# Attention and mixture of experts: second norm moved to DVE, pairs routed an iteration earlier, shared down products at the end on the output's PSUM banks

## The reference, cut to what matters

```python
x = x + attention(layernorm(x), ctx)              # 16 heads of 16, causal
h = layernorm(x)                                  # the second norm
scores = sigmoid(h @ gate_w.T)                    # 32 experts in 8 groups
# best 4 groups, best 8 experts of them; weights normalised, times 2.5
routed = sum_e weight_e * (silu(h @ w_gate_e) * (h @ w_up_e)) @ w_down_e
shared = (silu(h @ sh_gate.T) * (h @ sh_up.T)) @ sh_down.T     # two experts for all
out = x + routed + shared
```

## Time and profile before

| | |
|---|---|
| median of 3 runs | 600.98 us (599.45 to 603.95) |
| the profiled execution | 597.24 us, span 595.4 us |
| busy: PE, DVE, ACT, POOL | 455.0, 335.6, 208.9, 387.5 us |
| granted TensorE clock, mean | 0.858 |
| DMA | 85.08 MB, mean 143 GB/s |

### The profile page before, as it was taken

One profiled execution on the slowest core, in us unless ns is written; L12 is line 12 of the kernel. 1 busy time (PEld: TensorE's weight loads), 2 busy tenths in 40 slices (PEclk: granted clock), 3 DMA queues, 4 the chain that ended last, 5 costly groups with the idle time before them and its releaser, 6 DMA issues.

```text
span 595.4 us, 11968 instructions
## 1 busy us (share of the span) xinstructions
PE 455.0 (76%) x3114; PEld 344.2 (58%) x3114; DVE 335.6 (56%) x977; ACT 208.9 (35%) x595; POOL 387.5 (65%) x321
## 2 busy tenths in 40 slices
PE   2987996897585745971819998999989999998513
PEld 2985674665454523541507777777668867776302
DVE  5984999888867724531204555555546555555324
ACT  3452563343332300100004444444435544444201
POOL 7560122478877787757724888888868888888800
PEclk9998998866876756885858999999989999999955
DMA  6377600122222269389535888889888989888686
GB/s 206 94 286 224 224 4 2 30 80 79 68 79 80 78 197 395 93 231 252 159 97 96 146 144 139 143 141 145 140 132 142 146 138 151 144 141 138 82 243 210
DMA packets 88352, 85.08 MB, mean 143 GB/s; under 512 B 29164, under 2 KB 78956, under 8 KB 88288
## 3 DMA queue, kind: packets, MB, share of 16 engines
q0 software_dynamic: 27056, 32.01, 31.9%
q1 hardware_dynamic: 58928, 49.92, 30.2%
q10 hardware_dynamic: 2304, 2.37, 1.5%
HBM read 40.44 MB, written 43.80 MB: 141 GB/s over the span
## 4 chain that ended last, share of the span: by engine, by line
POOL 30%; issue 23%; PE 18%; DVE 11%; DMA 9%; SPq 8%; ACT 1%; POOLq 0%
POOL chosen_rows L365 21%; PE ps L971 7%; POOL sum L382 5%; DMA sum<-out_rows,rows 4%; DMA weight<-chosen_rows 3%; PE ps L987 3%; SPq L219 3%; POOL rec L356 2%; PE ps L749 2%; PE ps L963 2%; DVE prob L568 2%; SPq L299 2%; SPq L300 2%; DVE xn L514 1%; SPq L308 1%
## 5 line engine op out<-in xcount | busy, mean ns | idle before, releaser
L382 POOL DMA_INDIRECT sum<-out_rows,rows x131 | 202.1, 1542 | 61.0 <-issue 32.8
L365 POOL DMA_INDIRECT chosen_rows<-rec,dest x128 | 127.9, 999 | 43.0 <-issue 40.8
L971 PE MATMUL ps<-w_all,hx 128*128 x524 | 138.6, 388 | 0.0
L704 DVE SCALAR_TENSOR_TENSOR opened_t<-th,ps 128x128 f32<-128x128 f32 x131 | 37.7, 287 | 128.1 <-ACT th L475 127.2
L971 PEld LDWEIGHTS ps<-w_all,hx 128*128 128x128 f32 x524 | 91.2, 194 | 7.5
L987 PE MATMUL ps<-w_all,ax 128*128 x262 | 84.5, 404 | 1.6 <-ACT ax L481 0.9
L963 PE MATMUL ps<-cst,rows 128*128 128x128 f32 x262 | 53.1, 285 | 24.9 <-DMA weight<-chosen_rows 23.7
L471 ACT ACTIVATE hx<-ps 128x256 f32<-128x256 f32 x131 | 50.2, 383 | 35.5 <-PE ps L963 34.6
L475 ACT ACTIVATE th<-ps 128x128 f32<-128x128 f32 x131 | 36.3, 277 | 66.9 <-PE ps L971 66.4
L987 PEld LDWEIGHTS ps<-w_all,ax 128*128 128x128 f32 x262 | 43.8, 190 | 25.1 <-issue 21.0
L963 PEld LDWEIGHTS ps<-cst,rows 128*128 128x128 f32 x262 | 31.9, 144 | 43.3 <-DMA weight<-chosen_rows 35.5
(11 more groups left out here) (148 smaller groups left out, 670.1 us busy)
## 6 DMA issues: line engine op xcount, KB each, us to landing
rows<-chosen_rows SPq DMA_DIRECT2D x131, 128.5 KB
w_all<-w_exp SPq DMA_DIRECT2D x6, 1536.0 KB, 12.4
w_all<-sum SPq DMA_DIRECT2D x12, 384.0 KB, 7.1
sum<-pad_rec SPq DMA_DIRECT2D x2, 1600.0 KB
chosen_rows<-pad_rec SPq DMA_DIRECT2D x17, 144.5 KB, 6.2
chosen_rows<-pad_rec ACTq DMA_DIRECT2D x16, 144.5 KB, 5.3
w_all<-w_exp SPq DMA_DIRECT2D x1, 2304.0 KB, 12.7
weight<-chosen_rows SPq DMA_DIRECT2D x131, 0.5 KB
```

Source lines behind the costliest of these rows:

```text
L365: pool.indirect_dma_start(out=recs, out_offset=bass.IndirectOffsetOnAxis(ap=dest[:, B, r:r + 1], axis=0), in_=rec[:, B, :], in_offset=None ...
L382: pool.indirect_dma_start(out=sums[n], out_offset=bass.IndirectOffsetOnAxis(ap=rows[:, i % NROW, TOKEN:TOKEN + 1].bitcast(U32), axis=0), i ...
L704: v.scalar_tensor_tensor(opened_t[:, n, :], th[:, n, :], 1.0, ps[:, 2 + n, 0:FI], ALU.add, ALU.mult).then_inc(t_open, 1)
L971: last = t.matmul(ps[:, 2 + i % 2, 0:D].rearrange("p (a n) -> p a n", n=P), hx[:, i % 3, k * P:(k + 1) * P], weights(i)[:, k:2 * KC:2, :], ...
```

## The change

1. The second norm's subtraction and product go from POOL to DVE, behind `outputs_scaled` of the same step. POOL keeps the power. `send(B)` now follows the power of batch B+4. The token numbers in `rec` are written once ahead of the loop.
2. `route` runs at even steps from 4 on, `places` at even steps from 6 on, and PE's `count` at odd steps. The loop is one step shorter.
3. PE's transposes of `rec` go into the turning of batch B+3's probabilities, onto the free ends of banks 4 and 5; ACT copies them out between two probability copies. The residual waits no longer for the copy of the batch ahead.
4. The shared experts' down products and their additions on DVE go away from the middle. `sh_act` keeps all tokens, and at the end PE writes the down products, turned, into the eight PSUM banks of the output; the sums' blocks are added onto them by a product with the identity in place of a transpose. SP copies `x_all` to the first sum as soon as its residual is there.
5. `LOADED` is 8 in place of 4, for the zero rows and in the expert loop.

```diff
-LOADED = 4
+LOADED = 8
...
-        sh_act = keep("sh_act", [P, 2, 2, TG])
+        sh_act = keep("sh_act", [P, 2, T])
...
-        late_count = lambda p: 2 * p + 7 >= NB
+        late_count = lambda p: 2 * p + 6 >= NB
...
             experts_load(EARLY, EARLY + MIDDLE, w_middle)
+            def sum_start(c):
+                sp.wait_ge(x1_ready, BG * (c + 1))
+                sp.dma_start(sums[0][group_cols(c), :].rearrange("(b p) d -> p b d", p=S),
+                             x_all[:, c * BG:(c + 1) * BG, :]).then_inc(sum_begun, 16)
+
+            for c in range(NG - 1):
+                sum_start(c)
             sp.wait_ge(pv_psum, NB)
             for e in range(EARLY + MIDDLE, NE, 4):
                 experts_load(e, min(e + 4, NE), w_late)
 
-            def sum_start(c):
-                sp.wait_ge(sh_added, 2 * c + 2)
-                sp.dma_start(sums[0][group_cols(c), :].rearrange("(b p) d -> p b d", p=S),
-                             x_all[:, c * BG:(c + 1) * BG, :]).then_inc(sum_begun, 16)
-
-            sum_start(0)
+            sum_start(NG - 1)
             sp.wait_ge(pads_at, 1)
             padding(sp, mybir.EngineType.SP, 0)
-            for c in range(1, NG):
-                sum_start(c)
...
-            def second_norm(B):
+            def second_power(B):
                 pool.wait_ge(var2_ready, B + 1)
                 pool.tensor_tensor(rstd2[:, B, :], ve2[:, B, :], minus_half[:, 0:1], ALU.pow).then_inc(rstd2_ready, 1)
-                pool.wait_ge(rstd2_ready, B + 1)
-                if B == 0:
-                    pool.iota(rec[:, :, TOKEN].bitcast(I32), [[S, NB]], base=0, channel_multiplier=1).then_inc(numbers_ready, 1)
-                pool.tensor_scalar(rec[:, B, 0:D], x_all[:, B, :], mv2[:, B, 0:1], rstd2[:, B, :], ALU.subtract, ALU.mult).then_inc(h1_ready, 1)
...
+            pool.wait_ge(xt_lo_ready, NG)
+            pool.wait_ge(q_psum, KC * NG)
+            pool.iota(rec[:, :, TOKEN].bitcast(I32), [[S, NB]], base=0, channel_multiplier=1).then_inc(numbers_ready, 1)
             for B in range(NB):
-                second_norm(B)
-                if B >= 5:
-                    send(B - 5)
-            for B in range(NB - 5, NB):
+                second_power(B)
+                if B >= 4:
+                    send(B - 4)
+            for B in range(NB - 4, NB):
...
             def rows_turned(B):
                 a.wait_ge(ht_psum, B + 1)
-                a.activation(ht[:, :, batch_cols(B)], ps[:, 7, D:D + KC * S].rearrange("p (k q) -> p k q", k=KC), ACT.Copy).then_inc(ht_ready, 1)
+                a.wait_ge(pt_psum, min(RG * (B + 3) + 2, RG * NB))
+                a.activation(ht[:, :, batch_cols(B)], ps[:, 4:6, TG:TG + S], ACT.Copy).then_inc(ht_ready, 1)
...
+                if i >= 3:
+                    rows_turned(i - 3)
...
-                if 2 <= i < NB + 2:
-                    rows_turned(i - 2)
...
             def residual(B):
                 v.wait_ge(xb_ready, B // BG + 1)
                 v.wait_ge(proj_psum, B + 1)
-                if B:
-                    v.wait_ge(ht_ready, B)
...
+            def second_norm(B):
+                v.wait_ge(rstd2_ready, B + 1)
+                v.tensor_scalar(rec[:, B, 0:D], x_all[:, B, :], mv2[:, B, 0:1], rstd2[:, B, :], ALU.subtract, ALU.mult).then_inc(h1_ready, 1)
...
-            for i in range(NB + 5):
-                if 7 <= i < NB and i % 2 == 1:
-                    places((i - 7) // 2)
+            for i in range(NB + 4):
+                if 6 <= i < NB and i % 2 == 0:
+                    places((i - 6) // 2)
                 if i < NB:
                     maximum(i)
                     differences(i)
@@ -683,20 +677,20 @@
                     residual(i - 2)
                 if 1 <= i <= NB:
                     outputs_scaled(i - 1)
-                if i >= 5 and i % 2 == 1:
-                    route((i - 5) // 2)
-                if i >= NB and i % 2 == 0:
-                    places((i - 6) // 2)
+                if 2 <= i < NB + 2:
+                    second_norm(i - 2)
+                if 4 <= i < NB + 4 and i % 2 == 0:
+                    route((i - 4) // 2)
+                if i == NB:
+                    places(NPAIR - 3)
+                if i > NB and i % 2 == 1:
+                    places((i - 5) // 2)
...
+                if B >= 3 and r < KC:
+                    turn_rows(B - 3, r)
...
+                if 5 <= i < NB - 1 and i % 2 == 1:
+                    count((i - 5) // 2)
+                if i == NB:
+                    count(NPAIR - 3)
+                if i > NB and i % 2 == 1:
+                    count((i - 5) // 2)
+                if NB <= i < NB + 3:
+                    if i == NB:
+                        t.wait_ge(pt_ready, RG * NB)
+                    t.wait_ge(tanh_ready, i - 3)
+                    for k in range(KC):
+                        turn_rows(i - 3, k)
...
+            t.wait_ge(t_gated, NT)
+            t.wait_ge(o_ready, NT)
+            for q in range(len(BLOCKS)):
+                cols = part_cols(q)
+                for m in range(KC):
+                    for e in range(2):
+                        t.matmul(ps[:, 2 * q + m, 0:cols.stop - cols.start], wsh[:, e, 2 * D + m * P:2 * D + (m + 1) * P], sh_act[:, e, cols],
+                                 start=(e == 0), stop=False, skip_group_check=True)
             for q, (j0, j1) in enumerate(BLOCKS):
                 t.wait_ge(all_added, q + (2 if last_block(q) else 1))
                 for m in range(KC):
-                    for j in range(j0, j1 + (1 if last_block(q) else 0)):
+                    blocks = range(j0, j1 + (1 if last_block(q) else 0))
+                    for j in blocks:
                         n = min(P, T - j * P)
-                        last = t.transpose(ps[:, 2 * q + m, (j - j0) * P:(j - j0) * P + n], fetched(0)[0:n, j * D + m * P:j * D + (m + 1) * P],
-                                           ident[0:n, 0:n])
+                        last = t.matmul(ps[:, 2 * q + m, (j - j0) * P:(j - j0) * P + n], fetched(0)[0:n, j * D + m * P:j * D + (m + 1) * P],
+                                        ident[0:n, 0:n], start=False, stop=(j == blocks[-1]), skip_group_check=True)
                 last.then_inc(y_psum, 1)
```

54 lines of the change are left out of this document (9 added, 45 removed).

## The result

| kernel | median, us | lowest to highest | runs | profiled execution / span |
|---|---|---|---|---|
| before | 599.71 | 596.01 to 604.22 | 20 | 597.24 / 595.4 |
| after | 595.78 | 588.82 to 598.93 | 20 | 597.49 / 595.7 |

The ratio of after to before is 0.9911, 95% interval 0.9882 to 0.9939, where a gain of 14 us was forecast. The ratio compares the means of the executions within 1.5% of their kernel's fastest, without the profiled one, and comes to 5.3 us (3.7 to 7.1); the medians of all twenty differ by 3.9 us. The two profiled executions are of nearly the same length, one 2.5 us under its median, the other 1.7 us over it. The difference of the kernels cannot be read from the spans; it has to be read stage by stage.

What follows compares the result with a forecast made beforehand. POOL was taken to set the pace in sends and expert loop, DVE before the first send. -18.2 + 2.0 + 1.0 + 1.3 = -13.9 us, giving 587 on the median (own range 583 to 591); range for all 579 to 598.

Steps and rivals of the forecast that it cites:

- POOL's shorter batch: Send stage: with normalisation and its wait gone from POOL, a batch takes 10.98 us instead of 12.32.
- the 1.6 us added for collisions: Send stage: allowance for DVE's normalisation colliding with POOL's first send of a batch; 1.6 us, bounds 0 and 8.
- Rival 2: Send stage: DVE becomes the pace, its normalisation always held behind a send; +6 us on the sum, 593; chance 0.12.
- First send and batch 5: Start of sends: first send at 105.0 instead of 113.0; batch 5's power waits for DVE until 115.8.
- -18.2: Send stage: earlier first send and shorter batches end the last send at 285.0 instead of 303.2, -18.2 us.
- nine further batches of 10.98: Send stage: after batch 5's sends end at 126.9, the steady period puts the last power at 225.8.
- the idle with no releaser: Send stage: POOL's unexplained 5.25 us idle was kept, 4.95 beyond the normal gap, as the change does not touch it.
- The first block of eight, +2.0: Start of the expert loop: SP's register loads for eight tiles take 4.8 us instead of 2.87, exposed; +2.0 us.
- Blocks of eight in the loop, +1.0: Expert loop: each block's first tile comes later, using 2.0 of 2.9 us to spare; +1.0 us (0 to 16).
- rival 3: Expert loop: SP's blocks of eight starve POOL; 603 or 611 us; chance 0.14, a third of it over 607.
- The end: Tail: shared products hidden, last block's transposes become matmuls of two instructions each; +1.3 us (0 to 2.4).
- The middle, costed at nothing: Middle: shared products and additions ran beside POOL's sends, so removing them is worth nothing.

Runs made afterwards that it cites:

- experiment 3: Kernel after, still blocks of eight, with the places of pair 5 computed on DVE ahead of batch 14's second norm and pair 6's routing: 593.43 us, ratio 0.9900.
- experiment 4: Kernel after with blocks of four instead of eight and the places of pair 5 computed earlier on DVE: 585.08 us, ratio 0.9734.
- experiment 2: Kernel before with only LOADED changed, from 4 to 8: 610.29 us, ratio 1.0170.
- Experiment 5: Kernel after, still blocks of eight, with SP loading each block's registers ahead of its waits for landings: 589.49 us, ratio 0.9818.
- experiment 9: Kernel after, still blocks of eight, with 13 row buffers instead of 12: 589.67 us, ratio 0.9873.
- experiment 7: Kernel before with only the shared experts' part of the change (products at the end): 602.57 us, ratio 1.0027.
- experiment 11: Kernel after with blocks of four, pair 5's places early and loads ahead of waits, but the shared experts' part undone: 591.43 us, ratio 0.9827.
- experiment 1: Kernel after with LOADED back from 8 to 4: 589.88 us, ratio 0.9848.
- experiment 8: Kernel after with 32 small memsets of spare bytes on POOL ahead of its first power: 601.66 us, one run.

## Why the prediction was wrong

The direction and the mechanism of the gain were right, but the size was not: -3.9 us by the medians, -5.3 by the ratio, instead of -14. The time lies in the range (579 to 598) because the range is wide; the two steps that failed both erred to the same side. By its own steps:

- **POOL's shorter batch.** Right: 11.01 us against 10.98. The normalisation on DVE, 0.41 us, hardly collides with POOL: the first send of a batch takes 1.04 or 1.14 us, where the kernel before has 1.09 with no normalisation on DVE, and the send at 225.72, which meets none either, has 1.04. So at most 0.10 us of a send is a collision, the normalisation itself stays at 0.41 to 0.43 us (once 0.65, beside the very first send), and the 1.6 us added for collisions was too much. Rival 2 came only as three waits for DVE's variance, 2.12 us for batch 5 and 0.49 for batches 9 and 13. By the rule cited from the Trainium skill (page "SBUF — State Buffer", section "Who interferes with whom"), a DVE instruction in a 2-port mode and GpSimd exclude each other on a shared port pair for the whole instruction. These rows show no such block beside the sends.
- **First send and batch 5.** 106.29 instead of 105.0, and power 5 at 118.69 instead of 115.8. In the other profiles with the same attention part the first send is at 103.7 to 106.4 and the wait ahead of power 5 is 0.5 to 2.4 us; the step was sound to within that.
- **-18.2 was -11.8: "nine further batches of 10.98".** This is the first step that failed. It carried the steady period through to the last power without looking at the iterations after the last batch has entered the loop, where the order on DVE is another: there a norm that waits for POOL stands ahead of a routing and of the places POOL waits for, and 6.74 us are lost. The wait is in all five profiles with this attention part (6.73 or 6.74), and experiments 3 and 4 show its cause by removing it. Power 5, 2.9 us late, is the other part of the miss. Against it stand the collisions that did not come (1.6) and the idle with no releaser, rightly kept at 5.25, which was 3.44.
- **The first block of eight, +2.0.** Right in size: 5.3 us for eight against 3.0 for four, +2.3. At the first scatter-add +1.3 is left in this pair, and +2.5 in experiment 2. Experiment 5 hides it and gains 4.4.
- **Blocks of eight in the loop, +1.0: the second step that failed.** It measured some 5 us if the profiles' distances from the medians lie in the loop (9.2 between the two profiles), and 10.6 us with the first block in the kernel before. The mechanism is rival 3's, and its sign: POOL starves behind SP. The slack of 2.9 us was read at one late tile, 104. In the kernel before a result lies 0.8 to 1.5 us in the mean until POOL takes it over tiles 8 to 71, and 2.7 to 3.7 only from tile 72 on, so for half of the loop there was less than the 2.0 us to be taken. The late rows also meet PE three tiles earlier, ahead of the down product of tile 101; by itself this would not have changed the number, since tile 101 had 3.0 us in that trace. And the load was only counted as longer, not against the landings that hold SP before it comes to it; in experiment 9 one buffer more takes most of that hold and POOL's idle behind late results away. The further 5 us of waiting for landings of the sum in the profile after belong to neither step: kernels with fours have them too. The prediction's own mark ("the loop is longer than 250 us") was met: 253.9.
- **The end.** +1.6 against +1.3. Over the eleven kernels with the products at the end it is 31.7 to 35.3 us from the last scatter-add on, against 30.7, 30.7 and 31.7 for those without, so some 2 us. The products themselves (PE, 10.98 us from 558.73) were hidden, as said, at a granted clock of 1.00.

```profile
558.73 10.98 PE L996 MATMUL ps<-sh_act,w_shared 128*128 128x384 f32 x32 [0.61 <-DVE out_rows L710]
576.42 2.93 PE L1004 MATMUL ps<-cst,w_all 128*128 128x128 f32 x12 [6.71 <-DVE w_all L723]
...
588.13 3.85 PE L1004 MATMUL ps<-cst,w_all 128*128 128x128 f32 x16 [3.24 <-DVE w_all L723]
```

These are PE's rows of the kernel after that answer to the earlier trace rows: the shared products are over at 569.7, 6.7 us before the sums come, and the last block's matmuls take 3.85 us instead of 2.33 (3.5 forecast), at a granted clock of 0.60 instead of 0.50.

- **The middle, costed at nothing.** Right for this pair of kernels as far as experiment 7 can tell, but not a constant: the cover is the sends, and the profile of experiment 11 shows it gone when they end at 286 and the last addition at 297.7.

With the two failed steps mended, that is with the edits of experiments 1 and 3 in it, the change gives 585.08, ratio 0.9734: 14.6 us less than before (599.69 on that chip), or 16.0 by the ratio. The prediction's sum without its two terms for blocks of eight is -18.2 + 1.3 = -16.9, so the rest of it is sound to within some 2 us. Its last send ends at 285.87, where 285.0 was forecast.

## What to carry to other kernels

When a steady period is extended over a loop, list the order of the engines in its last iterations too: the stall sat in the one iteration whose order was different. When a transfer gets later, take its slack over the whole loop and not at one tile: here it was 1 us in the first half and 3 in the second. Look also at the first instruction that stands behind the transfer in any in-order queue, here a down product three tiles older. And judge a batch of work on an issuing queue by how far ahead that queue is when it starts it: with the same eight-tile loads the profiled loops took 252 to 260 us with 12 buffers and 246 with 13.

## What was not expected of the hardware

- The register loads of a block are not proportional to its tiles: 2.15, 2.95 and 5.3 us on SP for two, four and eight, 1.08, 0.74 and 0.66 a tile. With twos the loop takes 288.0 us instead of 250.9.
- PE has little to give in the loop. Over 340 to 540 us in the kernel before it is busy 190.56 of 200 us:

```profile
340.00:540.00 200.00, 190.56 (x970) 148.45 (x971) 104.26 (x323) 96.21 (x324) 163.18 (x107) 0.99 0.88 142
```

  (columns: window, length, busy us of PE, PEld, DVE, ACT and POOL, granted clock, DMA share, GB/s.) POOL's cycle of 1.85 us and SP's 1.8 a tile lie close beside it. With three engines within a few per cent of one pace, a stall of 2 us on one can hardly be made good before the next block comes; this is argued from the paces and not measured.
- The idle of 3.4 to 6.2 us ahead of send 93, at a fixed count and not at a fixed time, with nothing in the trace that ends it.
- POOL's idle behind the landings of its own scatter-adds, 1.2 to 6.9 us in a loop, whatever the size of the blocks.
- Executions of the same loop differ by 5 us and more (253.9, 258.7, 259.5: the kernel after, experiments 8 and 3), while their first scatter-adds can agree to a tenth (309.47 and 309.52 in the first two).
